# An attention and expert kernel on one core: six of the eight pieces of the experts' second product in split passes, and one weight split moved ahead of the gate gathers

## What is computed

```python
x = x + xattn(ctx, layernorm(x), mask, ...)    # 8 x 512 tokens of width 256; stage 1, not touched by the change
z = rmsnorm(layernorm(x)) * norm_weight        # 4096 tokens
logits = z @ router_weight.T + router_bias     # 16 experts
probs = softmax(logits)
_, idx = top_k(logits.T, 256)                  # each expert takes its 256 best tokens
xe = z[idx]                                    # (16, 256, 256)
h = gelu(xe @ fc1.T + fc1_bias)                # (16, 256, 1024)
y = h @ fc2.T + fc2_bias                       # (16, 256, 256): the second product
gates = take(probs.T, idx)
out = scatter_add(y * gates) / scatter_add(gates)
x = x + out
```

## Time and profile before

| | |
|---|---|
| time before, 3 runs | 1185.99 us median (1185.42 to 1186.02) |
| the profiled execution | 1185.55 us, of which its span 1183.7 us |
| PE busy | 1027.0 us, 87% |
| PEld busy | 634.1 us, 54% |
| DVE busy | 785.5 us, 66% |
| ACT busy | 671.8 us, 57% |
| POOL busy | 797.3 us, 67% |
| granted clock of TensorE | 0.939 mean; 1.00 in most of the expert stage |

### The profile page before, as it was taken

The page is one execution under the profiler, slowest core; times in us unless marked ns, Lnnn a source line. Parts: engine busy times, 40 slices in busy tenths (PEclk is TensorE's granted clock), DMA queues, the critical chain, the costliest instruction groups (busy, mean ns, idle before and its releaser), DMA issues.

```text
span 1183.7 us, 17328 instructions
## 1 busy us (share of the span) xinstructions
PE 1027.0 (87%) x5982; PEld 634.1 (54%) x5982; DVE 785.5 (66%) x1811; ACT 671.8 (57%) x1300; POOL 797.3 (67%) x891
## 2 busy tenths in 40 slices
PE   3669999999999999999999999998740298999996
PEld 2535445544644654554464465443220188999995
DVE  3666767876786886777677668775038765676752
ACT  5636756676576566657657655534414235656662
POOL 3305986797699589679769958969802248777773
PEclk9859999999999999999999999999965599999998
DMA  6020010011011002001110000000017227666752
GB/s 173 5 58 1 7 35 18 1 37 42 2 55 42 2 1 73 26 1 55 42 39 1 7 20 19 1 20 19 11 41 203 80 35 234 194 193 216 224 172 27
DMA packets 73479, 71.99 MB, mean 61 GB/s; under 512 B 38608, under 2 KB 67408, under 8 KB 69296
## 3 DMA queue, kind: packets, MB, share of 16 engines
q1 hardware_dynamic: 65392, 62.08, 16.4%
q0 software_dynamic: 6336, 8.70, 4.2%
q10 hardware_dynamic: 1664, 0.10, 0.1%
HBM read 56.97 MB, written 13.83 MB: 60 GB/s over the span
## 4 chain that ended last, share of the span: by engine, by line
PE 72%; POOL 10%; DVE 7%; issue 5%; ACT 4%; ACTq 1%; DMA 0%; POOLq 0%; DVEq 0%
PE bank L717 55%; PE pair_bank L717 12%; POOL prob_sum L1256 8%; ACT probs L1001 2%; DVE c_in L1559 2%; PE bank L790 2%; PE bank L742 2%; DVE masked_scores L1476 1%; PE bank L870 1%; POOL z_lo L1235 1%; PE bank L949 1%; DVE maxima L1469 1%; PE bank L778 0%; ACT c_in L1001 0%; POOL gate_rows L1315 0%
## 5 line engine op out<-in xcount | busy, mean ns | idle before, releaser
L1256 POOL TENSOR_TENSOR prob_sum<-prob_sum,probs 128x256 f32<-128x256 f32 x640 | 475.6, 775 | 80.9 <-ACT probs L1001 74.4
L1001 ACT ACTIVATE probs<-bank,mask_col 128x512 f32<-128x512 f32 x256 | 162.1, 686 | 109.7 <-PE bank L717 107.8
L1476 DVE CUSTOM_DVE_ANT_0 masked_scores<-pair_bank,mask_bias 128x512 bf16<-128x512 f32 x256 | 166.4, 688 | 81.7 <-PE pair_bank L717 81.5
L717 PE MATMUL bank<-probs,v_nat 128*64 128x512 f32 x768 | 205.1, 616 | 0.4 <-ACT probs L1001 0.4
L1469 DVE TENSOR_REDUCE maxima<-pair_bank 128x2 f32<-128x1024 f32 x64 | 78.3, 1224 | 47.2 <-PE pair_bank L717 47.2
L1001 ACT ACTIVATE probs<-bank 128x512 f32<-128x512 f32 x128 | 69.5, 594 | 66.0 <-PE bank L717 65.9
L717 PE MATMUL pair_bank<-k_hi,q_hi 64*128 64x512 f32 x384 | 93.2, 479 | 13.7 <-DVE maxima L1476 9.1
L717 PE MATMUL bank<-q_hi,k_hi 64*128 64x512 f32 x384 | 94.2, 484 | 10.7 <-ACT probs L1001 8.8
L1256 POOL TENSOR_TENSOR prob_sum<-probs 128x256 f32<-128x256 f32 x64 | 44.8, 731 | 82.1 <-ACT probs L1001 70.4
L1506 DVE RECIPROCAL bank<-bank 128x128 f32<-128x128 f32 x64 | 58.6, 944 | 58.4 <-PE bank L717 58.4
L717 PEld LDWEIGHTS bank<-q_hi,k_hi 64*128 64x128 f32 x384 | 37.2, 184 | 106.5 <-ACT probs L1001 55.3
(11 more groups left out here) (235 smaller groups left out, 2490.7 us busy)
## 6 DMA issues: line engine op xcount, KB each, us to landing
w_raw<-in_fc SPq DMA_DIRECT2D x16, 1024.0 KB, 4.8
w<-in_fc SPq DMA_DIRECT2D x16, 1024.0 KB, 6.3
c_in<-in_ctx SPq DMA_DIRECT2D x16, 384.0 KB, 3.4
x_in<-in_x SPq DMA_DIRECT2D x8, 512.0 KB, 4.9
out_x<-x_in SPq DMA_DIRECT2D x8, 512.0 KB, 3.5
rows_scratch<-xr_nat SPq DMA_DIRECT2D x8, 512.0 KB, 3.5
c_in<-in_ctx SPq DMA_DIRECT2D x16, 128.0 KB, 3.5
b_rows<-in_fc_bias SPq DMA_DIRECT2D x16, 128.0 KB, 5.6
```

Of the source, the lines that this page charges most:

```text
L717: return pe.matmul(out, lhsT, rhs, start=start, stop=stop, skip_group_check=True)
L1001: return act.activation(out, a, f, bias=bias, scale=scale)
L1256: last = tt(total[:, half], first[:, half], p[:, half], ALU.add)
L1476: last = dve.tensor_tensor_reduce(masked_scores[:, hh, :], pair_bank[:, hh, :], mask_bias[:, 512 * g:512 * (g + 1)], 1.0, MASKED, ALU.add, ...
```

## The change

`FS` goes from 4 to 6. In `expert_out` of experts 2 to 15 two more pieces of each c are made of three F32R matmuls in place of one float32 matmul; `w2_hi` and `w2_lo` are 128x1536 in place of 128x1024; `h_hi` and `h_lo` are made for pieces 4 and 5 too. `OUT_ORDER` for c = 1 starts with the pieces that are not split, now 6 and 7, before 4 to 7.

The plan of the first experts changes too. `split(2, 0)` goes from point 1 of expert 1 to behind the first `expert_out` of expert 0, ahead of `gather_gates(0)` and `(1)`, which also move there. In expert 1 `split(2, 1)` goes from point 9 to point 1, and the scatters of expert 0 from point 9 to point 10.

```diff
-SPLIT_FROM, FS = 2, 4
+SPLIT_FROM, FS = 2, 6
 OUT_ORDER = (tuple(range(FT)), tuple(range(FS, FT)) + tuple(range(FS)))
...
                 add("list_hot", 2, 0)
                 add("list_hot", 2, 1)
-                add("gather_gates", 0)
-                add("gather_gates", 1)
         for c in range(2):
             for n, f in enumerate(OUT_ORDER[c]):
                 add("expert_out", 0, c, f)
+                if c == 0 and n == 0:
+                    add("split", 2, 0)
+                    add("gather_gates", 0)
+                    add("gather_gates", 1)
...
-            if at == (9 if e == 1 else 4):
+            if at == (10 if e == 1 else 4):
                 for c in range(2):
                     add("scatter", e - 1, c)
-            if at == 1 and e == 1:
-                add("split", 2, 0)
-            if at == 9 and e + 1 < E:
+            if at == (1 if e == 1 else 9) and e + 1 < E:
                 add("split", e + 1, 1)
```

## The result

The changed kernel takes 1207.12 us (median of 4 runs, 1202.90 to 1209.27) where the kernel before took 1185.70 beside it. The ratio is 1.0179, 95% interval 1.0147 to 1.0210. Slower was forecast, but at 1189.5 us, and 1207 lies far outside the range of 1183.6 to 1193.0. The profiled execution took 1209.27 us, its span 1207.4, which is 23.7 us more than before.

The account below looks back on a forecast made before the run. TensorE bounds a steady expert, in loops with 0.2 us of slack. Start -1.2, expert 3 +0.4, four pairs +4.8, expert 12 +0.4, experts 13 to 15 -0.9: +3.5 on 1185.99 gives 1189.5 us, range 1183.6 to 1193.

Parts of the forecast that it names:

- Gain of the matmuls: In expert_out, three F32R matmuls replace one float32 matmul: 0.075 us a piece, 0.30 us an expert, 4.2 us in all.
- TensorE at list_spread: In even experts with a list, list_join stands behind h_lo(4), so TensorE waits 0.7 us ahead of list_spread.
- w2_lo behind GpSimd: At the expert border, the longer w2_lo ends 1.64 us behind GpSimd's subtraction, 0.54 us more than before.
- The odd expert: Delays in the loop of GpSimd, VectorE and TensorE make an odd expert with list_hot 0.8 us longer, net.
- the scatters start 1.25 later: In expert 9, GpSimd's border part 0.7 late plus w2_lo's 0.54 delay the scatters to 1086.1; the subtraction ends at 1092.4.
- up to 0.35: In expert 9, VectorE's hot_lo, pushed to about 1090.4, holds GpSimd for up to 0.35 us more.
- The clock: Rival: behind waits of about 1 us in odd experts TensorE's clock drops near 0.5; three add 4.7, 1194.2 us; 10%.
- The first experts: With the moved splits, TensorE's 3.61 us wait ahead of expert 2 goes, and expert 3 starts 1.2 us earlier.
- Step (a): In the first experts, GpSimd's moved subtraction at about 959.3 holds VectorE's hot_hi 2.3 us; hidden(2, 0) starts 1.7 earlier.
- (b): ScalarE gets w2 of expert 2 at 982.24 as before; w2_hi, half as long again, ends at 983.8, then GELUs.
- Experts 13 to 15: Without list_hot, and the last two without a GpSimd split beside w2_lo, each gains 0.3 us: -0.9 us together.
- The rule as the prediction cited it: GpSimd shares its SBUF interfaces with VectorE and collides with those of its instructions that have two SBUF inputs.

Follow-up runs that it names:

- the run with the tables early: Changed kernel with hot_hi and hot_lo (first part of list_hot) made in the even expert before: 1194.49 us, ratio 1.0072.
- after: The changed kernel itself, FS = 6 and the new plan of the first experts, against the kernel before: 1207.12 us, ratio 1.0179.
- split(2, 0) later: Changed kernel with all list_hot in even experts, list_join at point 4, list_spread at 8, split(2, 0) and gate gathers three pieces later: 1202.11 us, ratio 1.0143.
- more h alone: Kernel before with h_hi and h_lo made for six pieces while the products still use four: 1191.76 us, ratio 1.0038.

## Why the prediction was wrong

- **Gain of the matmuls: right.** 0.28 us an expert (12.69 to 12.41) against 0.30.
- **TensorE at list_spread: right.** 0.56 to 0.60 for 0.7, in all five even experts.
- **w2_lo behind GpSimd: right in kind.** It ends 1.6 us behind the subtraction (1067.59 against 1065.97) as forecast, and the long w2 by itself cost 0.24 an odd expert.
- **The odd expert: the step that failed** is "the scatters start 1.25 later ... and the subtraction ends at 1092.4". Its start of the scatters was right (0.85 us later than before, counted from the start of the expert; measured 0.84); it left their length at the earlier trace rows's 1.79, although it had hot_hi and hot_lo moved by 0.67 against them. It did have hot_lo hold GpSimd, but by "up to 0.35", and at the subtraction. What hot_hi and hot_lo held was the second scatter, by 1.81 us. Without that hold, in the run with the tables early, the odd expert is 13.44 us, the forecast's 13.5.
- **The clock: a rival had it, at too small a size.** It was given waits of 1 us and 10%. Border waits of 1.0 to 1.4 us left the clock at 1.00 in every profile. In after it was at its lower level behind all five border waits, of 2.66 to 3.02 us, at 1.5 to 2.6 us each. The two losses are one chain: 5 x 1.8 for the scatters and some 8.6 for the clock make 17.6 of the 20.2 us missed in the profile. The rest is the first experts and the end, less the 2.0 by which expert 0 started earlier. But such a wait does not bring the low clock each time: with the split pieces alone it did so in two of five, and that kernel's times were no better. How much of the median of 1207 is clock is therefore not shown.
- **The first experts: wrong by 4.3 us.** Step (a) had the subtraction at 959.3, "in its new place", holding hot_hi, and (b) had the gathers behind the gates' store as ones "that don't move". It ran at 957.1 and held the scaling of the gates, one instruction earlier. Counted from the start of expert 0, the first of these gathers started 2.5 us later (25.07 for 22.53), w2 of expert 2 reached ScalarE 2.95 later (38.28 for 35.33), and this used up the 2.0 us by which expert 0 had started earlier. list_count(2) waits 2.17 us and hidden(2, 0) starts at 981.43 for a forecast of 981.9, both near. list_spread came at 991.32 for 990.6, 0.7 late, and from there to expert 3 it took 9.26 us where the forecast had 7.7: the clock was low there, which no step had. 2.0, 0.7 and 1.6 are the 4.3.
- **Experts 13 to 15:** -0.1 for -0.9. Expert 14 waits 0.43 us for an h_lo in `expert_out`, which no row of before showed.

The range was too narrow mainly for this: it took its bounds from how late a piece starts, and, w2_lo aside, none from how long a piece takes once it stands beside other work, though the earlier trace rows had one instruction at 1.2 to 3.4 us.

## What to carry to other kernels

When a change shifts two engines against each other, list for each row in the loop what will run beside it afterwards, and give it the length that the same instruction has elsewhere beside such work. Here a shift of the tables by 0.7 us (more h alone) cost 0.3 us an odd expert, the stretched neighbour 1.8, and the low clock, where it came, 1.5 and more. TensorE was busy 100% of this stage while two other engines shared a loop with 0.2 us of slack, and shorter matmuls gained nothing until the loop was opened; opened, they only made up for what the change had added. So move work out of such a loop first, measure that, then shorten.

## What was not expected of the hardware

- An indirect DMA's issue on GpSimd, 1.58 us in even experts, took 1.79, 2.5, 3.26 and 3.60 us beside VectorE's one-hot tables, and 5.10 and 5.76 where h_lo stood across it as well. So the hold goes both ways. The Trainium skill (GPSIMD Engine Reference, Key points) speaks of contention in the shared SBUF interfaces; these rows agree.
- It isn't only instructions with two SBUF inputs that GpSimd's subtraction holds: a cast of 128x4 took 3.47 us, a scaling (hot_ids, one tensor input) 3.80, two scalings of y_out 2.40 for 0.60. The rule as the prediction cited it would have let these pass. The sentence of the Trainium skill (GPSIMD Engine Reference, Key points) is wider than that citation: it also names VectorE instructions in a 2-port perf mode. No trace here shows in which mode these ran.
- The length of a wait does not tell whether TensorE's clock falls behind it. It fell to 0.50 behind waits of 2.66, 4.06 and 5.20 us, to a mean of 0.59 over the 2.8 us behind a wait of 1.76, and in after behind one of 2.17. It stayed at 1.00 behind one of 2.37 (split(2, 0) later) and one of 2.47 (the new order alone), and with the split pieces alone behind one of 3.09 (ahead of expert 2) and three of 2.65 to 2.67. Stretches of that last run, behind the waits of 2.67 (expert 4) and 2.65 us (expert 6):

```profile
1020.21:1023.01 2.80, 2.80 (x45) 2.61 (x46) 2.80 (x1) 1.67 (x4) 2.77 (x2) 1.00 1.01 422
1050.38:1053.18 2.80, 2.80 (x12) 2.63 (x12) 2.80 (x1) 0.89 (x2) 2.77 (x2) 0.50 1.00 410
```

TensorE and VectorE are busy throughout both, and GpSimd and the DMA engines nearly so; what decides is not shown.
